# Second attention scores behind the next first scores in TensorE's queue

## The reference

```python
x = x + jnp.tanh(g_xattn[0]) * _L0_xattn_ref(_layernorm(x), ctx, ctx, ...)     # 16 heads of 16
...
scores = jnp.einsum('bhqd,bhkd->bhqk', q, k) / math.sqrt(D_K)
scores = jax.nn.softmax(scores, axis=-1)
col_sum = jnp.sum(scores, axis=2)
_, idx = jax.lax.top_k(col_sum, keep)                  # keep 90% of the key columns
mask = ...at[..., idx].set(1.0)
pruned = scores * mask[:, :, None, :]
return jnp.einsum('bhqk,bhkd->bhqd', pruned, v)
```

## Time and profile before

| what | us |
|---|---|
| time, median of 3 runs (lowest, highest) | 1215.02 (1215.01, 1220.33) |
| span of the profiled execution | 1211.1 |
| PE busy | 997.9 (82%) |
| Vector engine busy | 1013.7 (84%) |
| Scalar engine busy | 935.9 (77%) |
| steps 0 to 41, with the projections | 47.6 to 253.3 |
| steps 42 to 255, both passes | 253.3 to 738 |
| steps 256 to 297, second pass and the opening of the feed | 738 to 820.4 |
| rest of the feed | 820.4 to 1211.1 |

### The profile page before, as it was taken

The page is one execution under the profiler, slowest core; times in us unless marked ns, Lnnn a source line. Parts: engine busy times, 40 slices in busy tenths (PEclk is TensorE's granted clock), DMA queues, the critical chain, the costliest instruction groups (busy, mean ns, idle before and its releaser), DMA issues.

```text
span 1211.1 us, 17973 instructions
## 1 busy us (share of the span) xinstructions
PE 997.9 (82%) x5672; PEld 476.7 (39%) x5672; DVE 1013.7 (84%) x2009; ACT 935.9 (77%) x2135; POOL 163.6 (14%) x183
## 2 busy tenths in 40 slices
PE   7888999967777677777777778998999999999974
PEld 5554556511111111111111111335677777767652
DVE  6887677788889888889888887567999999999965
ACT  5456565489999999999999998776567667766744
POOL 2221231020000000000000000101232222222212
PEclk9999999989999999999999999989999999999985
DMA  9730653042211222111223101101111211110001
GB/s 308 180 114 1 200 149 104 19 123 38 39 27 34 45 45 45 33 31 29 44 46 80 33 20 35 37 9 40 53 36 36 62 44 36 49 48 27 18 18 35
DMA packets 77906, 71.80 MB, mean 59 GB/s; under 512 B 13754, under 2 KB 71412, under 8 KB 77812
## 3 DMA queue, kind: packets, MB, share of 16 engines
q1 hardware_dynamic: 77812, 70.65, 22.2%
HBM read 42.83 MB, written 27.28 MB: 58 GB/s over the span
## 4 chain that ended last, share of the span: by engine, by line
PE 42%; ACT 39%; issue 9%; DVE 9%; DMA 0%; POOL 0%; ACTq 0%; DVEq 0%
ACT ea L1322 19%; ACT prob L1336 15%; PE ps_a L1598 13%; PE ps_b L1556 8%; PE ps_v L1556 3%; DVE nmax L1223 2%; PE ps_c L1571 2%; PE ps_a L1607 2%; PE ps_c L1632 1%; PE ps_v L1195 1%; PE ps_b L760 1%; PE ps_v L735 1%; PE ps_b L701 1%; PE ps_b L1146 1%; PE ps_c L1179 1%
## 5 line engine op out<-in xcount | busy, mean ns | idle before, releaser
L1322 ACT ACTIVATE ea<-ps_a,nmax 128x512 f32<-128x512 f32 x512 | 362.7, 748 | 72.2 <-DVE nmax L1223 72.2
L1223 DVE TENSOR_REDUCE nmax<-ps_a 128x2 f32<-128x1024 f32 x256 | 313.7, 1225 | 52.7 <-PE ps_a L1146 51.4
L1336 ACT ACTIVATE prob<-ps_b 128x1024 f32<-128x1024 f32 x214 | 236.1, 1103 | 0.0
L1146 PE MATMUL ps_b<-q_st,k_st 52*128 52x512 f16 x512 | 105.8, 391 | 137.7 <-ACT prob L1336 129.6
L1146 PEld LDWEIGHTS ps_b<-q_st,k_st 52*128 52x128 f16 x512 | 26.1, 93 | 364.2 <-ACT prob L1336 303.9
L1598 PE MATMUL ps_a<-wgu,xT 128*128 128x352 f32 x512 | 166.2, 465 | 3.4 <-ACT xT L1761 2.1
L1195 PE MATMUL ps_v<-prob,v_in 128*16 128x512 f32 x1024 | 135.5, 600 | 11.9 <-DVE att L1290 11.5
L1179 PE MATMUL ps_c<-ea,rz 128*32 128x512 f32 x1024 | 137.2, 608 | 0.0
L1322 ACT ACTIVATION_READ_ACCUMULATOR ea<-ps_a,nmax 128x1 f32 x512 | 135.8, 265 | 0.0
L1598 PEld LDWEIGHTS ps_a<-wgu,xT 128*128 128x128 f32 x512 | 92.9, 191 | 48.9 <-issue 7.0
L1773 ACT ACTIVATE ea<-ps_a 128x352 f32<-128x352 f32 x128 | 59.7, 467 | 59.1 <-PE ps_a L1598 58.7
(11 more groups left out here) (279 smaller groups left out, 1685.8 us busy)
## 6 DMA issues: line engine op xcount, KB each, us to landing
k_scr<-k_p SPq DMA_DIRECT2D x24, 256.0 KB, 2.9
q_scr<-q_p SPq DMA_DIRECT2D x24, 256.0 KB, 2.8
q_st<-q_scr SPq DMA_DIRECT2D x32, 192.0 KB, 4.8
k_st<-k_scr SPq DMA_DIRECT2D x32, 192.0 KB, 5.0
c_in<-in_ctx SPq DMA_DIRECT2D x8, 512.0 KB, 4.4
x_in<-in_x SPq DMA_DIRECT2D x8, 512.0 KB, 5.9
v_scr<-v_s SPq DMA_DIRECT2D x8, 512.0 KB, 3.1
v_in<-v_scr SPq DMA_DIRECT2D x16, 256.0 KB, 3.2
```

The source lines that it names most:

```text
L1146: return e.matmul(bank, left[b][o:o + rows, r, t * P:t * P + P], right[b][o:o + rows, r], start=True, stop=True)
L1223: e.tensor_reduce(nmax[u % 2][:, t].rearrange("p (h r) -> p r h", h=2)[:, r], ps_a[:, z % 2 * 2:z % 2 * 2 + 2], AX_X, ALU.max, negate=True ...
L1322: e.activation(ea[c % RING][:, g % 4], ps_a[:, g % 4], ACT.Exp, bias=nmax[u % 2][:, t, n:n + 1], accum_out=tot[u % 2][:, t, n:n + 1]).then ...
L1336: e.activation(dst, ps_b[:, :, :], ACT.Exp).then_inc(s_prob, 1)
```

## The change

Inside a step of TensorE, the second scores are moved from the end to directly behind the first scores, and the half group number is one lower, so that a half group's second scores stand one first scores later than before:

```diff
         def step(z):
             if z < ALL_Z:
                 first(z)
+            b = within(z - LAG - 1, ALL_Z)
+            if b is not None:
+                second(b)
             if z % 2:
                 g = within((z - 5) // 2, ALL_G)
...
                 g = within((z - LAG - 4) // 2, ALL_G)
                 if g is not None:
                     values(g)
-            b = within(z - LAG, ALL_Z)
-            if b is not None:
-                second(b)
```

## The result

The changed kernel takes 1239.97 us (median of 4 runs, 1238.28 to 1242.28), the kernel before, on the same chip, 1215.21 (1215.01 to 1220.33). The ratio is 1.0195, with a 95% interval from 1.0172 to 1.0218. It is slower, as forecast, but by 24.8 us and not by 18.1: the median lies 6.9 us above the forecast of 1233.1 and 1.0 us above the upper end of the range.

A forecast was written before the change was run, and what follows sets the result against it. The prediction took the Scalar engine's exponentials to bound the attention body, with the cost in the tail. Its terms summed to +18.1 us, a span of 1229.2 and a median of 1233.1 us; range 1225 to 1239.

The forecast's parts named there:

- the body: Steps 48 to 255: the Scalar engine's exponentials set the pace, 2.25 us a half group; gain taken as 0.
- rival 2: The body is paced by starts of exponentials, held by the maxima: it gains 6.4 us, 1226.7 us; chance 0.05.
- The first steps: Steps 42 to 47: the new order takes away a wait of the Scalar engine, -0.7 us (0 to -0.7).
- W and T: Tail, first_product and x_T: two first_products cost 1.3 us each, part absorbed by x_T's wait for xg; +1.6 us.
- G(0): Tail, first gate_or_up, S(232) to S(234): second scores now stand just ahead of it; +1.7 us.
- The serial steps: Tail, eleven gate_or_up steps: second scores, probabilities, eviction, product run in a row, 3.36 us a step; 13.2 us in all.
- Rival 3: Something in the tail already held each step, so the serial steps cost half: about 1225 us; chance 0.06.
- S(240) to S(253) and the end: Late tail: +1.7 us around the Silu, +1.95 to S(248), +6.3 for five gate_or_up steps, -1.3 at the last probability.
- The clock, rival 1: TensorE falls to 1.2 GHz in the serial steps, 1.8 us each fall: 1235 to 1238.5 us; chance 0.13.
- Rivals 4 and 5: 4: body gains 7.1 us, tail under 1, 1208 to 1209; 5: body and tail cancel, 1212 to 1218; chance 0.03 each.

The follow-up runs named there:

- body_only: Kernel before with the new order only while first scores are issued (steps 42 to 254), old order in the tail: 1214.74 us, ratio 0.9995.
- wt_only: Kernel before, but in the tail up to n = 17 the second scores stand behind first_product and x_T: 1221.06 us, ratio 1.0049.
- wt_busy: wt_only plus 24 matmuls nobody reads, three ahead of the second scores at each even n from 2 to 16: 1220.11 us, ratio 1.0038.
- old_busy2: Kernel before plus unread matmuls in empty tail gaps: three at n = 5, 9, 11, 15, 17, nine at n = 30: 1214.09 us, ratio 0.9978.
- g_only: Kernel before, but in the tail the second scores stand behind gate_or_up in its sixteen steps: 1234.12 us, ratio 1.0156.
- old_busy: Kernel before plus unread matmuls in the tail, 27 at odd n of 1 to 17 and 8 ahead of S(244): 1217.01 us, ratio 1.0011.
- wt_busy2: wt_only plus 18 unread matmuls, only in the empty gaps at n = 6, 8, 10, 12, 14, 16: 1220.11 us, ratio 1.0025.
- wt_xm: wt_only with the Scalar engine's x_magnitude(0) moved ahead of prob(229): 1218.44 us, ratio 1.0022.
- evict_first: Changed kernel, but on the Scalar engine the eviction of each gate_or_up product stands ahead of the step's probabilities: 1225.88 us, ratio 1.0073.
- after_busy: Changed kernel plus unread matmuls, three each at n = 6, 8, 10, 12, 14, 16 and 8 ahead of S(244): 1237.01 us, ratio 1.0170.

## Why the prediction was right or wrong

**What bounds the kernel, and the body: right.** The Scalar engine's ends, not its starts, were the measure. body_only gives 0.9995, so rival 2 falls. The prediction cited the Trainium skill, "ScalarE: Activation LUTs", What ACT_TABLE_LOAD costs, for an estimate of 2.17 us a half group; with the maxima early the ends are still 2.25 to 2.26 us apart, so the trace does not agree with that estimate here.

**The first steps: right, hidden in the sum.** From the end of the exponential of step 42 to that of step 47 the traces fall into four groups, by order and by the length of the stretch at 1.2 GHz that lies there:

| order | stretch of 6.8 us | stretch of 10.3 us |
|---|---|---|
| before's | 11.96 to 12.11 us (before, wt_only, wt_busy, old_busy2) | 12.49 to 12.58 (g_only, old_busy, wt_busy2, wt_xm) |
| the new one | 11.35 (evict_first) | 11.89 to 11.90 (after, after_busy, body_only) |

Like against like the new order gains 0.6 to 0.8 us, forecast 0.7. In the pair before and after it is hidden, because after has the longer stretch (255.9 to 266.2 us, before 254.6 to 261.4). Of the +1.9 us up to S(214), 2.0 lie ahead of the change and 0.5 in this longer stretch, and 0.6 were gained.

**W and T: this term failed, 1.6 for 2.9 at the full clock.** The gaps at W were right to 0.01 us. Wrong was the overlap: the prediction let xg come 1.3 us later, because it followed the Vector engine's chain back to the copy of 756.39 alone, which lies ahead of the second W. A second chain, S(229), prob(229), L1752, ended at the same time in before (762.89 us, against 762.93 for the Vector engine's own work) and lies behind both W. It moved by 2.6 us and took T with it; nothing of the second W was absorbed. The trace of before showed both ends; the prediction followed only the one.

**G(0): 1.7 for 3.6.** The order of events was right, and the rest of the row is time at the low clock: from G at 777.97 to the next S it is 2.64 us for 1.38, and the S and V beside it were slower as well. No trace has this row at 2.4 GHz, so the 1.7 itself is not measured.

**The serial steps: right.** 3.39 us each on average for 3.36, 13.6 us in eleven steps for 13.2. evict_first shows the cause by taking it away. Rival 3 (half of it covered) falls with that.

**S(240) to S(253) and the end: right** within 0.7 us, the clock's fall in it included: after has one from 815.7 to 822.5 where before has it from 793.9.

**The clock, rival 1, happened elsewhere.** The prediction looked for it in the serial G steps, weighed 65% against 71% and 41%, and these steps did keep 2.4 GHz. The fall came in the W stretch, which no rival looked at, and took in V and W. It cost 4.1 us there, not the 1.8 forecast for one; by the rival's own rows, one and a half steps at 0.95 us, that price was 1.4. The share of a long stretch was not what told: wt_only had 79% from 745.3 to 753.2 and fell, evict_first had the same 79% and did not, and the serial steps with 67% did not. Beside this the Trainium skill, "TensorE: Matmul & The Clock Gate", A second HAM failure mode: psum-queue depth-cycling, says that frequent short idle times between groups of matmuls can make the clock swing; the prediction held the body against it. The traces agree with the page in part: three of four with the bare gaps fell and none of three with filled ones, while the body, the serial steps and evict_first show gaps that did no harm.

**The reference point.** The prediction put 3.9 us around the span by setting a profiled execution beside the median. Only about 2.1 us lie there; the other 1.8 are that this execution was shorter than the median, at a mean clock of 0.980. The sum was thus made on an execution at the good end and assumed the same clock for after. The range had room for falls in the serial steps only, at 1.8 us each. That the median still came within 1 us of its upper end is in part luck: the falls that brought it there are not those that the range was made for.

**Rivals 4 and 5** needed the tail to cost under 1 or 6 us; the whole change costs 19 us or more at either clock where the two can be compared, with nothing seen in the body. (Rival 3's 1225 was 1226.5 by its own terms; nothing hangs on it.)

What stays open: what decides when the clock falls. Each kernel has one trace, and the same order gave a fall in some and none in another. At 753 there was none in the three traces with filled gaps; at 794 stretches of 3.4 and 6.8 us come with the same order; near 766 some traces fall with either order.

## What to carry over

In this in-order queue a swap of two short instructions cost nothing that could be seen where another engine's ends set the pace (ratio 0.9995), and 1.2 us a step where it closed a ring in which S, its probability, the eviction and G wait for each other in turn; look for a product with two banks (here G) whose eviction stands, on the other engine, behind the instruction that consumes what now stands ahead of it (here the probability of S). Follow a wait back along every chain that feeds it, also those that end just in time and show no idle time. Judge the Scalar engine's pace by the ends of its records. Where a change opens short gaps on TensorE, allow for a stretch at the lower clock wherever gaps open, and compare variants at equal mean clock, and in more than one trace, before explaining a few microseconds.

## What the runs showed that was not expected

- The kernel before, a program of one core, takes from 1212.8 to 1221.9 us as its mean granted clock goes from 0.980 down to 0.972.
- Twenty-four matmuls that nobody reads, put where TensorE waits anyway, make the kernel faster (old_busy2, ratio 0.9978, 0.9966 to 0.9989).
- The Scalar engine's records of the same exponentials grew from 748 to 1179 ns on average, and those of the 128x1024 probability from 1103 to 1607, with the ends 2.25 to 2.26 us apart in both: it is the start of a record that moved, to a time when earlier work was unfinished. The busy sum of L1322 rose from 362.7 to 472.7 us with no work added.
